# Graph layers in seven-tile chunks over pairs of PSUM banks instead of half chunks in five banks

## The chip, the core and the metric

The kernel runs on one core of a Trainium2 chip. The metric is the device time of one execution in microseconds. Five engines work side by side, each in the order of its own queue, and wait for each other by semaphores: PE (matmuls; its weight loads are listed as PEld), ACT, DVE, POOL and SP, which here only issues transfers.

## What is computed

6250 nodes of 128 features pass through a layer norm, a graph attention layer and three message-passing layers over 200000 edges. The change concerns the three layers:

```python
for i in range(3):
    msg = relu(x[src] + edge_attr)
    aggr = segment_sum(msg, dst, num_segments=6250)
    h = x + aggr
    h = relu(batch_norm(h @ W1[i] + b1[i]))
    h = batch_norm(h @ W2[i] + b2[i])
    x = relu(h) if i != 2 else h
```

## The kernel before

**Tiling.** The nodes stand in 49 blocks of 128. Most edges, sorted by target, form 36 groups. A stage ahead of the layers gives each edge of a group a slot by the block of its source, so that a group is 49 tiles of 128 slots, one tile for each source block, and all its targets lie in one window of 128 nodes. Seven tiles are a chunk, seven chunks a group. A chunk is worked on in two halves, of four and of three tiles; half h belongs to chunk h // 2. The last edges do not go this way: they form 69 units of 7 x 128 edges, about two units to a group, whose source rows POOL gathers one by one.

**A chunk, step by step.** SP loads the attributes of the slots into SBUF (the tile is called `sums`).

- The copy (`seed`, ACT, line 1158) puts the attributes of a half into a PSUM bank.
- The gather (`gather`, PE, line 2049) adds the rows of x: three matmuls to a tile, one for each bf16 part of x, with a one-hot of the sources.
- The relu (`message`, ACT, line 1166) writes the message from PSUM to SBUF.
- The rest (`split_message`, DVE, line 1692) subtracts that from the relu in PSUM, so that the message stands in two parts. In layer one (n = 0) chunks 1, 3 and 5 go without it: there the message is kept whole.
- The one-hot of the targets (`point_targets`, DVE, line 1685) compares an iota with `dl_slot`. The iota stands in PSUM bank 5.
- The sum (`sum_half`, PE, line 2073, or 2076 for whole messages) multiplies message and one-hot, summed over the group in bank 7.

At the group's end ACT copies the window from bank 7 (line 1173), PE turns it (line 2087), and DVE adds it to the nodes (line 1701).

**A unit.** POOL sends seven indirect gathers (line 941), paced by a count of finished sums; DVE adds attributes and rows (line 1715) and makes a one-hot (line 1708); ACT does the relu (line 1178); PE sums (line 2097), in fourteen recorded matmuls; DVE adds the window (line 1722). A table of half numbers says after which half each engine does this.

**What sets the order.** The order is written out by hand in a `group_of` for each engine; groups 2 to 34 run in a hardware loop. A bank is reused by the half that `BANK` puts there next, four, five or seven halves later. ACT runs `message(h)` and then `seed(h + 3)`; PE runs the gather of half h + 3 (at h = 0 those of halves 3 and 4, and none at h = 1) and then the sum of half h. A copy waits until the bank's last user is through (its rest, or its relu for a whole message). A relu also waits until the place in SBUF for its message was emptied by the sum of the chunk that had it.

In layer one DVE also makes the one-hots of the sources (line 1678), three chunks ahead, and POOL scatters sixty late tiles of attributes (line 884) between its gathers; in layers two and three the source one-hots come back from memory by SP.

## Time and profile before

| | us |
|---|---|
| median of three runs | 5063.85 (5047.44 to 5081.66) |
| span of the profiled execution | 4090.3 |
| layer one, from 1838 to 2592 us of the span | 754 |
| layer two, from 2639 to 3319 us | 680 |
| layer three, from 3372 to 4044 us | 672 |

The span runs from the first to the last instruction of one profiled execution. Busy time counts an engine's instructions; an operation's end can overlap the start of the next on the same engine. In a row of the timeline, "x21" is a run of 21 instructions, and the square brackets say how long the engine stood idle before it and what ended that. In a row of groups the time behind the bar is the idle time before the group, with its releasers; "issue" is time in which the engine waited for nothing that the profile shows. PEclk is the granted clock of PE as a share of 2.4 GHz. The rows that are used stand further down.

### The profile page before, as it was taken

Reading aid. Unit: us, or ns where it says so; the run is one execution under the profiler, and the core shown is the slowest. Engines: PE = TensorE matmul, PEld = TensorE weight load, DVE = VectorE, ACT = ScalarE, POOL = GpSimd, SP = SyncE. Lnnn points to the kernel's source line nnn. Section 1 sums busy time; section 2 is a strip of 40 time slices with the busy share of each in tenths; the row PEclk is TensorE's granted clock in tenths of the full one; section 3 lists DMA queues with packets and bytes.
Section 4 is the critical chain, followed back from the end, with each engine's and each line's share of the span. In section 5 each row is a group of like instructions: output and inputs, shape, how many; then the busy total and the mean of one; then the engine's idle time right before and its main releaser. Section 6 shows DMA issues by size and latency. Waiting matters only on the chain.

```text
span 4090.3 us, 151537 instructions
## 1 busy us (share of the span) xinstructions
PE 3879.3 (95%) x50507; PEld 3753.5 (92%) x50510; DVE 3556.7 (87%) x6832; ACT 3072.5 (75%) x7847; POOL 2859.0 (70%) x2594
## 2 busy tenths in 40 slices
PE   3899997999999999989999999899999989999998
PEld 3899996999999999979999999699999969999996
DVE  7799985777777777779999999799999989999997
ACT  4799994677777777777777777678888867887886
POOL 0288885777777777756777777277777736777773
PEclk7788888999999999999999999899999999999999
DMA  9989889998888888868999999589999958999995
GB/s 140 216 291 305 286 277 297 234 248 253 247 250 250 253 247 250 247 211 293 337 338 334 333 329 333 171 300 310 323 310 318 317 176 288 318 319 311 314 316 186
DMA packets 710002, 1132.45 MB, mean 277 GB/s; under 512 B 157402, under 2 KB 535084, under 8 KB 709564
## 3 DMA queue, kind: packets, MB, share of 16 engines
q1 hardware_dynamic: 493068, 787.26, 57.5%
q10 hardware_dynamic: 133200, 176.14, 17.7%
q0 software_dynamic: 83552, 166.66, 12.7%
q8 instruction: 110, 1.80, 0.2%
q14 instruction: 72, 0.59, 0.0%
HBM read 883.83 MB, written 246.33 MB: 276 GB/s over the span
## 4 chain that ended last, share of the span: by engine, by line
PE 84%; DVE 5%; DMA 3%; issue 2%; ACT 2%; SPq 2%; POOL 1%; ACTq 0%; DVEq 0%; PEld 0%; POOLq 0%
PE ps L2049 20%; PE ps L1955 15%; PE ps L2073 14%; PE ps L1942 12%; PE ps L2097 7%; PE ps L2076 4%; PE ps L1883 2%; PE ps L1903 2%; PE ps L1904 2%; PE ps L1891 2%; DMA unit_x<-gin_rows,unit_src 2%; PE ps L2144 2%; PE ps L2087 1%; POOL unit_x L941 1%; DMA h_rows<-att 1%
## 5 line engine op out<-in xcount | busy, mean ns | idle before, releaser
L941 POOL DMA_INDIRECT unit_x<-gin_rows,unit_src x1449 | 1446.6, 998 | 487.8 <-issue 318.4
L878 POOL DMA_INDIRECT attr_by_slot<-abuf,ridx x1020 | 1286.0, 1261 | 455.9 <-issue 308.5
L2049 PE MATMUL ps<-x_parts,src_turned 128*128 128x128 bf16 x15876 | 1137.0, 222 | 21.5 <-ACT ps L1158 18.5
L2049 PEld LDWEIGHTS ps<-x_parts,src_turned 128*128 128x128 fp8e4 x15876 | 948.6, 99 | 67.8 <-issue 25.3
L1158 ACT ACTIVATE ps<-sums 128x512 f32<-128x512 f32 x1512 | 825.8, 546 | 125.9 <-DVE all_split_msg L1692 70.7
L1066 ACT ACTIVATE val<-ps,val 128x128 f32<-128x128 f32 x2597 | 717.9, 375 | 182.6 <-DVE val L1519 182.6
L1685 DVE TENSOR_TENSOR dst_hot<-ps,dl_slot 128x896 fp32r<-128x896 f32 x756 | 817.8, 1082 | 3.5 <-issue 0.4
L1955 PE MATMUL ps<-val,src_hot 128*128 128x129 f32 x5194 | 691.6, 282 | 3.0 <-ACT val L1066 2.5
L2073 PE MATMUL ps<-all_split_msg,dst_hot 128*128 128x256 f32 x3528 | 648.8, 304 | 13.2 <-DVE all_split_msg L1692 12.6
L1166 ACT ACTIVATE all_split_msg<-ps 128x512 fp32r<-128x512 f32 x1008 | 543.7, 539 | 146.0 <-PE ps L2049 113.7
L1692 DVE SCALAR_TENSOR_TENSOR all_split_msg<-ps,all_split_msg 128x512 fp32r<-128x512 f32 x1008 | 609.1, 617 | 14.0 <-ACT all_split_msg L1166 11.5
L1955 PEld LDWEIGHTS ps<-val,src_hot 128*128 128x128 f32 x5194 | 617.5, 192 | 3.7 <-ACT val L1066 2.8
L1942 PE MATMUL ps<-h_win,turned_hot 128*128 128x130 bf16 x7791 | 583.6, 221 | 24.3 <-DVE turned_hot L1445 18.6
L1942 PEld LDWEIGHTS ps<-h_win,turned_hot 128*128 128x128 bf16 x7791 | 502.5, 97 | 30.5 <-issue 19.1
L2073 PEld LDWEIGHTS ps<-all_split_msg,dst_hot 128*128 128x128 f32 x3528 | 479.1, 191 | 17.9 <-issue 10.1
L1944 PE MATMUL ps<-s_parts,turned_hot 128*128 (+1 forms) x2597 | 433.8, 167 | 0.0
L1511 DVE TENSOR_TENSOR src_hot<-iota_one,low 128x768 f32<-128x768 f32 (+1 forms) x441 | 415.7, 943 | 0.0
L2097 PE MATMUL ps<-unit_hot,unit_attr 128*128 128x64 f32 x2898 | 345.7, 271 | 0.0
L2097 PEld LDWEIGHTS ps<-unit_hot,unit_attr 128*128 128x128 f32 x2898 | 341.0, 192 | 0.0
L1507 DVE TENSOR_REDUCE z<-ps 128x6 f32<-128x24 f32 (+1 forms) x490 | 83.6, 179 | 252.6 <-PE ps L1944 251.6
L1445 DVE TENSOR_SCALAR turned_hot<-turned_hot,lane_one 128x1536 bf16<-128x1536 bf16 (+1 forms) x441 | 267.4, 606 | 17.5 <-DMA turned_hot<-rows_by_block 17.5
L1715 DVE TENSOR_TENSOR unit_attr<-unit_attr,unit_x 128x896 f32<-128x896 f32 x207 | 225.8, 1091 | 37.6 <-DMA unit_x<-gin_rows,unit_src 37.2
(268 smaller groups left out, 5787.5 us busy)
## 6 DMA issues: line engine op xcount, KB each, us to landing
sums<-attr_by_slot SPq DMA_DIRECT2D x756, 448.0 KB
turned_hot<-rows_by_block ACTq DMA_DIRECT2D x392, 384.0 KB
attr_by_slot<-zeros SPq DMA_DIRECT2D x36, 3136.0 KB
unit_attr<-in_edge_attr SPq DMA_DIRECT2D x204, 448.0 KB
abuf<-in_edge_attr SPq DMA_DIRECT2D x68, 960.0 KB
src_turned<-src_hots SPq DMA_DIRECT2D x504, 112.0 KB
src_row<-rows_by_group SPq DMA_DIRECT2D x252, 112.0 KB
src_hots<-src_turned SPq DMA_DIRECT2D x252, 112.0 KB
```

The source lines that it names most:

```text
L878: pool.indirect_dma_start(out=attr_table, out_offset=bass.IndirectOffsetOnAxis(ap=ridx[:, g, t0 + t:t0 + t + 1], axis=0), in_=abuf[:, k % ...
L941: pool.indirect_dma_start(out=unit_x[:, half_place(k), t, :], out_offset=None, in_=gin_rows[n], in_offset=bass.IndirectOffsetOnAxis(ap=uni ...
L1066: ins = act.activation(val[:, slot, t, 0:D], given(slot, t)[:, 0:D], ACT.Copy, scale=val[:, slot, t, D:SUM])
L1158: act.activation(ps[:, BANK[h], 0:tiles * D].rearrange("p (b d) -> p b d", d=D), attr[:, first:first + tiles, :], ACT.Copy).then_inc(s_see ...
L1166: act.activation(to, ps[:, BANK[h], 0:tiles * D].rearrange("p (b d) -> p b d", d=D), ACT.Relu).then_inc(s_msg, 1)
L1685: vec.tensor_tensor(dst_hot[:, HOT[c], :, :], iota_ps.unsqueeze(1).to_broadcast([P, G_TILES, P]), dl.rearrange("p o b -> p (o b)").unsquee ...
L1692: vec.scalar_tensor_tensor(split_msgs[n][:, SPLIT_PLACES[n][c], 1, inner, :], ps[:, BANK[h], 0:tiles * D].rearrange("p (b d) -> p b d", d= ...
L1942: pe.matmul(to[:, 0:ROW], turned_hot[:, 0, at:at + P], window_of(g)[:, part * ROW:(part + 1) * ROW], start=(t % 3 == 0 and part == 0), sto ...
L1955: ins = pe.matmul(ps[:, 6, 0:SUM], src_hot[:, slot, t, :], val[:, slot, t, :], start=(c == 0 and t == 0), stop=(c == A_CHUNKS - 1 and t == ...
L2049: ins = pe.matmul(ps[:, BANK[h], k * D:(k + 1) * D], src_turned[:, b * P:(b + 1) * P], x_parts[:, part, b, :], start=False, stop=(k == til ...
L2073: ins = pe.matmul(ps[:, 7, 0:2 * D].rearrange("p (k d) -> p k d", d=D), dst_hot[:, HOT[c], b % G_TILES, :], split_msgs[n][:, SPLIT_PLACES[ ...
L2097: ins = pe.matmul(ps[:, 6, 0:U_WINDOW], unit_attr[:, half_place(k), t, :], unit_hot[:, half_place(k), t, :], start=(t == 0), stop=(t == ti ...
```

## The change

A chunk is no longer halved on its way through PSUM. It lies across two neighbouring banks, and three such pairs take turns by `PAIR`: chunks 0 to 6 use pairs 0, 1, 2, 0, 1, 2, 1, so that chunk 6 follows chunk 4 in pair 1, and chunk 1 of the next group follows chunk 6. Copy, relu and rest become one operation of 896 columns each. PE gathers a whole chunk, two chunks ahead; the sum still runs in two halves, but waits once for the whole chunk, and the unit of a chunk and the turning of the window still stand between or behind these halves. The six banks leave none for the iota, so both one-hots (targets and units) read it from SBUF.

```diff
-BANK = (4, 2, 3, 0, 1, 2, 3, 4, 0, 1, 2, 3, 0, 1)
-IOTA_BANK = 5
+PAIR = (0, 1, 2, 0, 1, 2, 1)
 HOT = (0, 1, 2, 3, 0, 1, 2)
...
-G_LEAD = 3
-AHEAD = ((3, 4), ()) + tuple((h + G_LEAD,) for h in range(2, G_HALVES))
-SEED_LEAD = 3
+G_LEAD = 2
...
-RELU_AT = {6: 0, 13: 1}
+RELU_AT = {3: 0, 6: 1}
...
-WINDOW_OUT_AT = 2
+WINDOW_OUT_AT = 1
...
+        def chunk_ps(c):
+            return ps[:, 2 * PAIR[c]:2 * PAIR[c] + 2, :].rearrange("p b e -> p (b e)")[:, 0:G_TILES * D]
...
+                def seed(i, c):
+                    act.wait_ge(s_attr[c], 16 * (n * BUCKETS + i + 1 + cleared(c)))
+                    before = pair_user(c)
                     if not (isinstance(i, int) and i == 0 and before < 0):
-                        if before % G_HALVES // 2 in SPLITS[n]:
+                        if before % G_CHUNKS in SPLITS[n]:
                             act.wait_ge(s_low, lows_done(n, i, before))
                         else:
-                            act.wait_ge(s_msg, halves_before + G_HALVES * i + before + 1)
-                    act.activation(ps[:, BANK[h], 0:tiles * D].rearrange("p (b d) -> p b d", d=D), attr[:, first:first + tiles, :], ACT.Copy).then_inc(s_seed, 1)
+                            act.wait_ge(s_msg, chunks_done + G_CHUNKS * i + before + 1)
+                    act.activation(chunk_ps(c), attr[:, parts_of(c), :].rearrange("p b d -> p (b d)"), ACT.Copy).then_inc(s_seed, 1)
...
+                def message(i, c):
+                    act.wait_ge(s_gath, chunks_done + G_CHUNKS * i + c + 1 + G_CHUNKS)
+                    act.wait_ge(s_used, halves_before + G_HALVES * i + 2 * place_user(n, c) + 2 + G_HALVES)
...
+                    act.activation(to.rearrange("p b d -> p (b d)"), chunk_ps(c), ACT.Relu).then_inc(s_msg, 1)
...
-                    for h in range(G_HALVES):
...
+                        message(i, c)
+                        if c == WINDOW_OUT_AT and not (isinstance(i, int) and i == 0):
                             keep_window(i - 1)
...
+                        if c + G_LEAD < G_CHUNKS:
+                            seed(i, c + G_LEAD)
                         elif more:
...
+                            seed(i + 1, c + G_LEAD - G_CHUNKS)
...
-                    vec.tensor_tensor(dst_hot[:, HOT[c], :, :], iota_ps.unsqueeze(1).to_broadcast([P, G_TILES, P]),
+                    vec.tensor_tensor(dst_hot[:, HOT[c], :, :], iota_one[:, :].unsqueeze(1).to_broadcast([P, G_TILES, P]),
...
+                def split_message(i, c):
+                    vec.wait_ge(s_msg, chunks_done + G_CHUNKS * i + c + 1)
...
+                    vec.scalar_tensor_tensor(low_of, chunk_ps(c), 0.0, hi, ALU.max, ALU.subtract).then_inc(s_low, 1)
...
-                    vec.tensor_tensor(unit_hot[:, half_place(k), 0:tiles, :], iota_ps[:, 0:U_WINDOW].unsqueeze(1).to_broadcast([P, tiles, U_WINDOW]),
+                    vec.tensor_tensor(unit_hot[:, half_place(k), 0:tiles, :], iota_one[:, 0:U_WINDOW].unsqueeze(1).to_broadcast([P, tiles, U_WINDOW]),
...
-                        if c in SPLITS[n]:
-                            split_message(i, h)
+                        if h % 2 == 0 and c in SPLITS[n]:
+                            split_message(i, c)
...
-                        for k in AHEAD[h]:
...
+                        if h % 2 == 0 and h // 2 + G_LEAD < G_CHUNKS:
+                            gather(i, h // 2 + G_LEAD)
+                        elif h % 2 == 0 and more:
+                            gather(i + 1, h // 2 + G_LEAD - G_CHUNKS)
                         sum_half(i, h)
```

**ACT, the end of a group in the loop of layer three.** Lines with ACTIVATE are the operations; `rows_gathered` counts gathers, `message_rest_ready` rests, `message_used` sums; `slots_cleared_then_slot_attr_loaded1` says that chunk 1's attributes are loaded, and `ps<-sums` is a copy, `all_split_msg<-ps` a relu. Before (relu of half 12, copy of half 1 of the next group, relu of half 13, copy of half 2, relu of the unit):

```order
L1166 ACTIVATE all_split_msg<-ps 128x512 [waits message_used,rows_gathered]
L1155 REGISTER_ALU
L1158 ACTIVATE ps<-sums 128x384 [waits message_rest_ready]
L1163 REGISTER_ALU
L1166 ACTIVATE all_split_msg<-ps 128x384 [waits message_used,rows_gathered]
L1155 REGISTER_ALU [waits slots_cleared_then_slot_attr_loaded1]
L1158 ACTIVATE ps<-sums 128x512 [waits message_rest_ready]
L1177 REGISTER_ALU
L1178 ACTIVATE unit_attr<-unit_attr 128x896 [waits unit_raw_ready]
L1211 REGISTER_ALU
L1211 COMPARE_AND_BRANCH
```

Now (relu of chunk 6, copy of chunk 1 of the next group, relu of the unit; the loop then begins again, with the relu of chunk 0):

```order
L1157 REGISTER_ALU
L1158 REGISTER_ALU [waits rows_gathered]
L1160 ACTIVATE all_split_msg<-ps 128x896 [waits message_used]
L1151 REGISTER_ALU [waits slots_cleared_then_slot_attr_loaded1]
L1154 ACTIVATE ps<-sums 128x896 [waits message_rest_ready]
L1171 REGISTER_ALU
L1172 ACTIVATE unit_attr<-unit_attr 128x896 [waits unit_raw_ready]
L1204 REGISTER_ALU
L1204 COMPARE_AND_BRANCH
```

The copy that stood here for half 2 waited for the rest of half 11; the copy of chunk 1 waits for the rest of chunk 6, whose relu stands one row of work ahead of it, and the unit's relu and the next chunk's relu stand behind it.

**PE around the unit of chunk 4, same loop.** `attributes_in_bank` counts copies, and `h_windows_loaded6` says here that chunk 6's source one-hots are loaded. Before (gather of half 11, sum of half 8, the unit):

```order
L2041 REGISTER_ALU
L2049 MATMUL ps<-x_parts,src_turned 128x128 [waits attributes_in_bank]
L2049 MATMUL ps<-x_parts,src_turned 128x128 x8
L2057 REGISTER_ALU
L2061 REGISTER_ALU [waits message_rest_ready]
L2073 MATMUL ps<-all_split_msg,dst_hot 128x256 [waits dst_hot_ready]
L2073 MATMUL ps<-all_split_msg,dst_hot 128x256 x3
L2095 REGISTER_ALU [waits unit_added,unit_hot_ready,unit_message_ready]
L2097 MATMUL ps<-unit_hot,unit_attr 128x64 [waits window_added]
L2097 MATMUL ps<-unit_hot,unit_attr 128x64 x6
```

Now (gather of chunk 6, first half of sum 4, the unit, second half of sum 4):

```order
L2028 REGISTER_ALU [waits h_windows_loaded6]
L2037 MATMUL ps<-x_parts,src_turned 128x128 [waits attributes_in_bank]
L2037 MATMUL ps<-x_parts,src_turned 128x128 x20
L2046 REGISTER_ALU
L2049 REGISTER_ALU [waits message_rest_ready]
L2061 MATMUL ps<-all_split_msg,dst_hot 128x256 [waits dst_hot_ready]
L2061 MATMUL ps<-all_split_msg,dst_hot 128x256 x3
L2083 REGISTER_ALU [waits unit_added,unit_hot_ready,unit_message_ready]
L2085 MATMUL ps<-unit_hot,unit_attr 128x64 [waits window_added]
L2085 MATMUL ps<-unit_hot,unit_attr 128x64 x6
L2061 MATMUL ps<-all_split_msg,dst_hot 128x256 x3
```

The gather of chunk 6 stands ahead of all of sum 4. Before, the gather ahead of sum 4 was that of half 11, the second of chunk 5, and chunk 6's two gathers (halves 12 and 13) stood behind the unit, ahead of the sums of halves 9 and 10.

**DVE, the one-hots and rests of chunks 4 and 5, same loop.** Before (one-hot of chunk 4, rest of half 8, the unit's one-hot, rest of half 9, one-hot of chunk 5 behind):

```order
L1685 ISA [waits message_used]
L1685 TENSOR_TENSOR dst_hot<-ps,dl_slot 128x896
L1691 REGISTER_ALU
L1692 SCALAR_TENSOR_TENSOR all_split_msg<-ps,all_split_msg 128x512 [waits message_ready]
L1706 REGISTER_ALU
L1708 ISA [waits unit_used]
L1708 TENSOR_TENSOR unit_hot<-ps,unit_dl 128x448
L1691 REGISTER_ALU
L1692 SCALAR_TENSOR_TENSOR all_split_msg<-ps,all_split_msg 128x384 [waits message_ready]
L1684 REGISTER_ALU
L1685 ISA [waits message_used]
L1685 TENSOR_TENSOR dst_hot<-ps,dl_slot 128x896
```

Now (one-hot of chunk 4, rest of chunk 4, the unit's one-hot, one-hot of chunk 5 behind):

```order
L1678 ISA [waits message_used]
L1678 TENSOR_TENSOR dst_hot<-iota_one,dl_slot 128x896
L1682 REGISTER_ALU
L1684 SCALAR_TENSOR_TENSOR all_split_msg<-ps,all_split_msg 128x896 [waits message_ready]
L1697 REGISTER_ALU
L1699 ISA [waits unit_used]
L1699 TENSOR_TENSOR unit_hot<-iota_one,unit_dl 128x448
L1677 REGISTER_ALU
L1678 ISA [waits message_used]
L1678 TENSOR_TENSOR dst_hot<-iota_one,dl_slot 128x896
```

The rest stands at the place of its first half, and both one-hots read `iota_one`, which lies in SBUF, in place of `ps`.

## Rows read from the trace of the kernel before

**Rows 1.** The page's first row: span and number of instructions.

```profile
span 4090.3 us, 151537 instructions
```

**Rows 2.** Stretches, the layers: length; busy PE, PEld, DVE, ACT, POOL; clock, DMA, GB/s.

```profile
1838.00:2592.00 754.00, 745.61 (x8923) 730.58 (x8924) 694.84 (x1041) 551.68 (x1117) 555.09 (x550) 0.99 0.94 325
2639.00:3319.00 680.00, 664.68 (x8168) 644.97 (x8168) 652.61 (x1007) 544.04 (x1117) 489.39 (x490) 0.99 0.90 307
3372.00:4044.00 672.00, 659.18 (x8107) 638.92 (x8107) 646.99 (x1000) 538.76 (x1107) 490.38 (x489) 0.99 0.89 304
```

**Rows 3.** Line 1701, layer two, fourteen window adds: min/median/max ns, first and last start.

```profile
L1701 DVE TENSOR_TENSOR agg<-agg,ps x14: 273/274/285, 2862.1 to 3102.2; 128x128 f32 x14
```

**Rows 4.** Groups by line, layer two, POOL: busy, mean ns, idle before, its releasers.

```profile
L941 POOL DMA_INDIRECT unit_x<-gin_rows,unit_src x483 | 480.7, 995 | 166.8 <-issue 103.6 <-PE ps L2073 62.0 <-DVE unit_attr L1715 1.2
```

**Rows 5.** Timeline, layer two, PE: start us, length us, operation, count.

```profile
3002.17 1.67 PE L2097 MATMUL ps<-unit_hot,unit_attr 128*128 128x64 f32 x14
3003.67 1.34 PE L2049 MATMUL ps<-x_parts,src_turned 128*128 128x128 bf16 x21
3004.82 1.07 PE L2073 MATMUL ps<-all_split_msg,dst_hot 128*128 128x256 f32 x7
3005.73 0.68 PE L2049 MATMUL ps<-x_parts,src_turned 128*128 128x128 bf16 x9
3006.22 0.72 PE L2073 MATMUL ps<-all_split_msg,dst_hot 128*128 128x256 f32 x4
3006.78 0.84 PE L2049 MATMUL ps<-x_parts,src_turned 128*128 128x128 bf16 x12
...
3007.87 0.68 PE L2049 MATMUL ps<-x_parts,src_turned 128*128 128x128 bf16 x9
```

**Rows 6.** Groups by line and form, layer two, ACT.

```profile
L1158 ACT ACTIVATE ps<-sums 128x512 f32<-128x512 f32 x252 | 151.1, 600 | 34.6 <-DVE all_split_msg L1692 34.5
L1166 ACT ACTIVATE all_split_msg<-ps 128x512 fp32r<-128x512 f32 x252 | 148.9, 591 | 38.0 <-PE ps L2049 19.6 <-issue 15.8
L1158 ACT ACTIVATE ps<-sums 128x384 f32<-128x384 f32 x252 | 124.6, 494 | 0.0
L1166 ACT ACTIVATE all_split_msg<-ps 128x384 fp32r<-128x384 f32 x252 | 122.9, 488 | 36.0 <-PE ps L2049 34.3 <-issue 1.7
L1178 ACT ACTIVATE unit_attr<-unit_attr 128x896 f32<-128x896 f32 x69 | 65.3, 947 | 14.9 <-DVE unit_attr L1715 14.8
```

**Rows 7.** Timeline, layer two, DVE.

```profile
3000.74 1.08 DVE L1685 TENSOR_TENSOR dst_hot<-ps,dl_slot 128x896 fp32r<-128x896 f32 x1
3001.74 1.15 DVE L1692 SCALAR_TENSOR_TENSOR all_split_msg<-ps,all_split_msg 128x512 fp32r<-128x512 f32 x2
3002.80 1.08 DVE L1685 TENSOR_TENSOR dst_hot<-ps,dl_slot 128x896 fp32r<-128x896 f32 x1
...
3005.42 1.08 DVE L1685 TENSOR_TENSOR dst_hot<-ps,dl_slot 128x896 fp32r<-128x896 f32 x1
...
3007.15 1.08 DVE L1715 TENSOR_TENSOR unit_attr<-unit_attr,unit_x 128x896 f32<-128x896 f32 x1
```

**Rows 8.** Timeline, layer two, POOL, two gathers in succession.

```profile
3005.94 0.95 POOL L941 DMA_INDIRECT unit_x<-gin_rows,unit_src  x1 [0.31 <-PE ps L2073]
3007.19 1.86 POOL L941 DMA_INDIRECT unit_x<-gin_rows,unit_src  x1 [0.30 <-PE ps L2073]
```

**Rows 9.** Attention stage, 750 to 1810 us: three groups by line, one timeline row.

```profile
L878 POOL DMA_INDIRECT attr_by_slot<-abuf,ridx x776 | 820.8, 1058 | 236.5 <-issue 236.5
...
L1511 DVE TENSOR_TENSOR src_hot<-iota_one,low 128x768 f32<-128x768 f32 x364 | 348.9, 959 | 0.0
L1445 DVE TENSOR_SCALAR turned_hot<-turned_hot,lane_one 128x1536 bf16<-128x1536 bf16 x362 | 222.1, 613 | 0.0
...
1207.36 0.96 POOL L878 DMA_INDIRECT attr_by_slot<-abuf,ridx  x1 [0.30 <-issue]
```

**Rows 10.** Groups by line, layer one, DVE: the one-hot of the sources.

```profile
L1678 DVE TENSOR_SCALAR src_turned<-src_row,lane_one 128x896 fp8e4<-128x896 uint8 x251 | 176.5, 703 | 2.4 <-DMA src_row<-rows_by_group 2.0 <-issue 0.5
```

126 lines of the change are left out of this document (48 added, 78 removed).

## The prediction

> **What bounds the kernel now.** I took the whole time first, then the three layers, then what each engine does in one group. The profiled execution spans 4090.3 us [rows 1]; the median of the runs is 5063.85 us, so 973.5 us lie around the span, and I leave them unchanged. The three layers fill 754, 680 and 672 us of the span [rows 2]; the change touches nothing else, apart from a few waits before them.
>
> In the layers PE is busy 98 to 99% of the time, DVE 92 to 96%, ACT 73 to 80%, at a granted clock of 0.99, the 2.4 GHz level [rows 2]. A group of the second layer takes (3102.2 - 2862.1) / 13 = 18.5 us [rows 3]. DVE works 652.6 / 36 = 18.1 us of it: two engines are nearly full, so no wait of DVE can be hidden for long.
>
> POOL looks idle and is not. In layer two it sends 483 gathers (14 in a full group) of 0.995 us on average [rows 4], and 0.3 us passes before each, even when nothing is waited for [rows 9]: 14 x 1.30 = 18.2 us of 18.5 in a full group. Of the 166.8 us that it stood idle before them, 483 x 0.3 = 145 are this step; 22 us in the whole layer are room. In layer one two scatters of late edges come on top: 16 operations of 1.01 us (555.09 / 550 [rows 2]) and 0.3 make 20.9 us, which is all of 754 / 36 = 20.9.
>
> **The change, part by part.** I write g for the 21 gather matmuls of a chunk, S for its rest on DVE, P for its one-hot on DVE, and a number for the chunk.
>
> *PE, a gain.* No matmul is added or removed. A gather of 21 with its sum of 7 takes 3005.73 - 3003.67 = 2.06 us; the same work as 9, 4, 12 and 3 takes 3007.87 - 3005.73 = 2.14 [rows 5]. Before, one chunk of a group already runs whole, so the gain is 6 x 0.08 = 0.48 us a group, 52 us over 108 groups; in layer one it may be less. This holds only if PE stays the bound.
>
> *ACT, less work.* From 384 to 512 columns an operation grows by 0.106 us (copy) and 0.103 us (relu) [rows 6]. Three more such steps give 0.92 and 0.90 us for 896 columns. The row of an 896-wide relu, 0.947 us, bounds a whole operation in one piece. No row shows one across two banks; if the crossing cost a second start, the price would be that of the two halves of now, 1.09 and 1.08 us, and nothing would be gained. ACT works about 2.5 us a group less, but it was not full: nothing on the path, except where DVE waits for it.
>
> *DVE, about 0.4 us a group less.* Two halves of S run as a pair in 1.15 us. A P of 896 takes 1.08 us, and its successor starts 1.00 us after it [rows 6, 7]. I price S like P: 0.06 to 0.07 us saved per chunk. DVE's own work becomes 18.1 - 0.4 = 17.7 us a group. The copy of the iota into PSUM, once a layer, is worth under 1 us.
>
> *A wait at the end of the group.* Chunk 1 of the next group uses the same pair as chunk 6. ACT stands in order: relu 6, copy 1' (waits for S6), relu of the unit, relu 0'. DVE runs S6, P0, S0, and S0 needs relu 0'. From the end of S6: copy 0.92, unit relu 0.95, relu 0.90, and 0.03 at either end for a semaphore (an estimate), less twice the 0.08 by which an operation of DVE overlaps the next [rows 7], which I take for ACT too: 2.7 us. DVE has only P0 to put there, 1.0 us. It waits 1.7 us. Behind S0 in DVE's queue stand all further one-hots and rests, and PE needs those. Before, the copy at that place waited for the rest of half 11 and not of half 13.
>
> *A wait in the middle.* Chunk 6 uses the pair of chunk 4, and relu 6 also needs the message place that sum 4 empties. In layers two and three, from the end of S4: copy 6 with its semaphores 0.98, g6 1.15, first four of sum 4 0.56, the unit's fourteen 1.50 (they stand between the halves of sum 4), last three 0.5 (three sevenths of a sum's 1.07), relu 6 0.90, semaphores 0.06: 5.7 us until S6 can start [rows 5, 6]. DVE's own work there is a unit one-hot (half as wide as P, an estimate of 0.55), P5, S5, P6 and the unit's add: 4.6 us. It waits 1.1 us. In layer one chunk 6's place was last used by chunk 2, so this wait is absent.
>
> Sum for layers two and three: 17.7 + 1.7 + 1.1 = 20.5 us a group in place of 18.5. That is 2.0 x 36 = 72 us a layer, 144 for both. PE's 18.0 us of work fits inside. In layer one DVE's 694.8 / 36 = 19.3 [rows 2], less 0.2 for four chunks merged, with 2.7 - 1.0 - 0.7 = 1.0 of wait (a source one-hot of 0.70 us fills part [rows 10]), makes 20.1: under the 20.9 of now, so the order costs nothing there.
>
> *The iota back in SBUF.* P and the unit's one-hot read dl_slot or unit_dl from SBUF already, so now both inputs lie in SBUF. DVE itself pays nothing: the unit's add, with both inputs in SBUF, takes the same 1.08 us [rows 7]. POOL pays. A gather takes 0.95 us; one that began 0.04 us after such an add took 1.86 us, and ended 0.82 us after the add did [rows 7, 8]. It was held until DVE was done. The gather before it began 0.52 us after a P and took 0.95: with the iota in PSUM, P holds nobody.
>
> The Trainium skill ("SBUF — State Buffer", "Who interferes with whom") states that a DVE operation with two SBUF inputs contends with a GpSimd instruction that reads SBUF, and that the one issued second fully blocks; it speaks against this edit. The trace agrees for the add; that it also holds for the new P, no row of this kernel's layers shows.
>
> Seven P of 1.08 and two unit one-hots of 0.55 make 8.7 us a group in which a gather can now be held, 42% of 20.5. The price per gather is bounded from two rows. Upper end: a gather falls at random and waits half an operation, 0.42 x 0.5 = 0.21 us. Lower end: in the attention stage POOL also runs without pause, next to a one-hot of the very form P now has and a second one-hot of 0.61 us, together (348.9 + 222.1) / 1060 = 54% of the time; its scatters average 1.058 us against 0.96 free [rows 9]. That is 0.10 us at 54%, so 0.08 at 42%. For 14 gathers: 1.1 to 2.9 us, so POOL needs 19.3 to 21.1 us a group. The sum of the waits, 20.5, lies inside: POOL's delay runs beside them, and I add nothing for it there.
>
> Layer one has no wait of order to cover it, and POOL nothing to spare. Its 16 operations with 0.08 to 0.21 more (8.7 of 20.9 is the same share) need 1.3 to 3.4 us a group. I take 1.6, nearer to the lower end, whose row has the same form of one-hot: 1.6 x 36 = 58 us, from 47 to 122.
>
> *Sum:* 144 + 58 = 202 us. The span becomes 4292, the time 5064 + 202 = 5266 us.
>
> **The rivals.**
>
> 1. *POOL becomes the bound.* Where DVE runs S and P without a pause, a held gather ends 0.82 us after P, and the next starts 0.3 later, 1.12 after P's end. By then the next P runs (S takes 1.0), so POOL is held again: one gather a chunk instead of two, until DVE pauses. Its 18.2 of 18.5 us speak for this, the attention stage against it, where a larger share cost it only 0.10 us. At the upper end layers two and three take 21.1 us (2.6 x 36 = 94 each) and layer one 122: +310, 5374 us. If one gather a group more is lost, at 1.25 us, for which DVE's add then waits, that is 135 us on top: 5509.
>
> This rival is the rule of the Trainium skill ("SBUF — State Buffer", "Who interferes with whom") taken as the bound; the add's row agrees with its mechanism, and no row yet with its size here.
>
> 2. *The pipeline closes up and PE stays the bound: not slower.* One mechanism decides it: whether copy 1' and copy 6 find their pair free by the time PE has other work. DVE would have to be 1.7 us ahead at the end of the group. Its load of 96% speaks against it: it idles 27 us in a whole layer [rows 2]. If it is so, the gain of PE stands: -52, 5012 us. POOL must then fit in 18 us too, which needs a price under 0.05 per gather.
>
> 3. *The waits are half as long,* since a full chunk of lead lets DVE catch up in the stretch between S0 and S4, and POOL pays the lower end: 72 + 47 = +119, 5183 us.
>
> **How the numbers follow.** The waits of order as summed, with POOL beside them: 0.46 (5200 to 5330). Rival 1: 0.26. Rival 3: 0.15, with a tail towards no change. Rival 2: 0.13, half of it below -1%, since -52 us is just about that. A measurement of this kernel tells about 1% (51 us) from no change. Faster by over 1% (below 5013): 0.06. Within 1%: the other half of rival 2 and a quarter of rival 3, 0.11. Slower: 0.83. The range runs from 5100, in the tail of rival 3, to 5420, in the upper half of rival 1; rival 2 and the ends of the other two, 0.2 in all, lie outside.
>
> **What would show it.** Right: groups of layers two and three about 20.5 us apart; PE busy well under 98% there; DVE's rest waiting for ACT's relu about 36 times a layer for over 1 us, and ACT's copy waiting for the rest; gathers at 1.08 us or more. Also right: a gather of 21 and a sum of 7 still 2.06 us. Wrong: PE at 98% again (rival 2), or DVE's unit add waiting for gathers most of all, with POOL idle for nothing but its 0.3 (rival 1). Were the 896-wide operations much dearer over two banks than 1.08 and 0.95 us, the sum would fail from the other side.

## The result and the profile after

The changed kernel takes 5346.66 us (median of 4 runs, 5334.68 to 5376.3), the kernel before 5061.52 (4 runs, 5047.44 to 5081.66) on the same chip: 1.057 times as long, with an interval of 1.052 to 1.062. That is 285 us more, where the prediction had 202, and inside its range.

Its profiled execution spans 5339.4 us, which is nearly its whole time. The profile of before that stands ahead of the prediction spans 4090.3 us [rows 1] of a time of some 5060. A second profile of the same kernel before, taken for this study, spans 5011.8 us in a run of 5013.5. So nothing of size lies around the span there. The time of the execution behind the first profile is not on record; by its rows it was faster than any that was timed. From here on, "the kernel before" is this second profile, and [rows 2 to 4] are kept for what they led to.

The three layers of the second profile of before, by windows (length; busy time and count of PE, PEld, DVE, ACT, POOL; granted clock, DMA share, GB/s):

```profile
2260.00:3200.00 940.00, 813.28 (x8958) 747.68 (x8959) 720.88 (x1067) 559.11 (x1129) 561.32 (x550) 0.99 0.85 264
3250.00:4090.00 840.00, 719.26 (x8024) 653.30 (x8023) 658.74 (x1007) 536.35 (x1098) 480.79 (x483) 0.98 0.74 244
4140.00:4980.00 840.00, 720.33 (x8068) 654.87 (x8067) 662.28 (x1012) 537.68 (x1102) 483.66 (x485) 0.98 0.74 244
```

And of the changed kernel:

```profile
2280.00:3273.00 993.00, 822.51 (x8939) 791.68 (x8939) 701.12 (x904) 516.67 (x626) 651.17 (x555) 0.91 0.81 251
3330.00:4285.00 955.00, 774.65 (x8097) 744.06 (x8095) 651.44 (x749) 502.62 (x609) 533.23 (x490) 0.87 0.65 218
4340.00:5300.00 960.00, 778.13 (x8119) 744.76 (x8118) 657.11 (x758) 505.64 (x614) 527.51 (x490) 0.87 0.65 216
```

DVE, ACT and POOL of the kernel before work about as long as in [rows 2], PE 8% longer (719 us for 665), and this in layers that are 160 us longer: PE is busy 86% of the second layer and DVE 78%, not 98 and 96. No engine is full. With the change PE is busy 81%, DVE 68%, and the clock granted is 0.87 in place of 0.98.

The window adds of layer two give the length of a group, as [rows 3] did: first the kernel before, then the changed one (count; min/median/max ns; first and last start).

```profile
L1701 DVE TENSOR_TENSOR agg<-agg,ps x36: 275/278/290, 3263.7 to 4073.7; 128x128 f32 x36
```

```profile
L1692 DVE TENSOR_TENSOR agg<-agg,ps x36: 277/289/291, 3362.9 to 4285.8; 128x128 f32 x36
```

(4073.7 - 3263.7) / 35 = 23.1 us a group before, (4285.8 - 3362.9) / 35 = 26.4 after: 3.2 us more. The groups by line and shape of the changed kernel in layer two, of ACT, DVE and POOL (busy us, mean ns; idle before, its releasers), answer to [rows 4, 6, 7]:

```profile
L1154 ACT ACTIVATE ps<-sums 128x896 f32<-128x896 f32 x249 | 228.8, 919 | 150.9 <-DVE all_split_msg L1684 113.5 <-issue 37.4
L1160 ACT ACTIVATE all_split_msg<-ps 128x896 fp32r<-128x896 f32 x251 | 228.7, 911 | 286.9 <-PE ps L2061 192.5 <-PE ps L2037 48.9 <-remote 40.7
...
L1684 DVE SCALAR_TENSOR_TENSOR all_split_msg<-ps,all_split_msg 128x896 fp32r<-128x896 f32 x251 | 273.3, 1089 | 136.3 <-ACT all_split_msg L1160 112.6 <-issue 21.4 <-DVE agg L1731 0.8
L1678 DVE TENSOR_TENSOR dst_hot<-iota_one,dl_slot 128x896 fp32r<-128x896 f32 x250 | 271.5, 1086 | 0.0
...
L939 POOL DMA_INDIRECT unit_x<-gin_rows,unit_src x483 | 524.8, 1087 | 401.0 <-PE ps L2061 247.8 <-issue 81.3 <-remote 65.6
```

Copy 0.919, relu 0.911, rest 1.089, one-hot 1.086, gather 1.087: each price of the prediction is met. What is new stands behind the second bar. Copies wait for the rest, relus for the sums, the rest for relus.

PE's side of layer two, kernel before first, gives the whole account:

```profile
L2049 PE MATMUL ps<-x_parts,src_turned 128*128 128x128 bf16 x5154 | 380.9, 221 | 51.7 <-issue 45.3 <-ACT ps L1158 3.9
L2073 PE MATMUL ps<-all_split_msg,dst_hot 128*128 128x256 f32 x1730 | 324.7, 308 | 48.9 <-issue 24.4 <-DVE all_split_msg L1692 15.1 <-ACT window_out L1173 8.6
L2097 PE MATMUL ps<-unit_hot,unit_attr 128*128 128x64 f32 x966 | 121.2, 272 | 13.9 <-issue 13.5
```

```profile
L2037 PE MATMUL ps<-x_parts,src_turned 128*128 128x128 bf16 x5229 | 386.2, 236 | 169.1 <-ACT ps L1154 147.5 <-issue 20.9
L2061 PE MATMUL ps<-all_split_msg,dst_hot 128*128 128x256 f32 x1759 | 325.3, 322 | 7.9 <-issue 5.6 <-DVE all_split_msg L1684 2.2
L2085 PE MATMUL ps<-unit_hot,unit_attr 128*128 128x64 f32 x966 | 149.3, 321 | 0.0
```

The window of layer two is 115 us longer. PE idles 60 of them: by these rows 117 more before gathers, which wait for the copy of attributes, and 55 less before sums and unit sums. The other 55 are busy time (774.65 - 719.26): the same unit sum takes 321 ns a matmul where it took 272. The two windows end differently, so here is the stretch from the first to the last window add as well, kernel before first:

```profile
3263.70:4073.70 810.00, 695.08 (x7851) 636.77 (x7849) 638.31 (x971) 521.86 (x1068) 473.68 (x476) 0.98 0.75 249
3362.90:4285.80 922.90, 750.56 (x7823) 721.29 (x7821) 629.60 (x728) 483.29 (x585) 515.86 (x475) 0.87 0.65 217
```

113 us more, of which 57 are idle time of PE and 55 busy time, for as many matmuls within 0.4%. The clock records of the trace say where the busy time comes from: in this stretch the change was granted 1.2 GHz for 246 us, in 49 pieces, the kernel before for 31 us, in five.

Some of the growth is the chip's. The second profile of before comes from a chip on which its run took 5013.5 us, the change from one on which the kernel before takes 5061.5: 1% more, about 8 us a layer.

One group shows both halves. The timeline of the changed kernel at chunk 6 (start, length, operation, idle before):

```profile
3602.89 0.29 DVE L1692 TENSOR_TENSOR agg<-agg,ps 128x128 f32 x1 [2.03 <-remote]
...
3603.12 1.09 DVE L1678 TENSOR_TENSOR dst_hot<-iota_one,dl_slot 128x896 fp32r<-128x896 f32 x1
3604.13 1.08 DVE L1684 SCALAR_TENSOR_TENSOR all_split_msg<-ps,all_split_msg 128x896 fp32r<-128x896 f32 x1
...
3605.25 0.92 ACT L1154 ACTIVATE ps<-sums 128x896 f32<-128x896 f32 x1 [2.30 <-issue]
...
3606.32 2.40 PE L2037 MATMUL ps<-x_parts,src_turned 128*128 128x128 bf16 x21 [2.67 <-ACT ps L1154]
...
3608.47 1.20 PE L2061 MATMUL ps<-all_split_msg,dst_hot 128*128 128x256 f32 x4
...
3609.47 3.08 PE L2085 MATMUL ps<-unit_hot,unit_attr 128*128 128x64 f32 x14
...
3612.31 0.99 PE L2061 MATMUL ps<-all_split_msg,dst_hot 128*128 128x256 f32 x3
...
3612.69 0.22 DVE L1713 TENSOR_TENSOR agg<-agg,ps 128x64 f32 x1 [4.57 <-PE ps L2085]
...
3613.34 0.92 ACT L1160 ACTIVATE all_split_msg<-ps 128x896 fp32r<-128x896 f32 x1 [5.52 <-PE ps L2061]
...
3614.93 1.09 DVE L1684 SCALAR_TENSOR_TENSOR all_split_msg<-ps,all_split_msg 128x896 fp32r<-128x896 f32 x1
3615.93 1.08 DVE L1678 TENSOR_TENSOR dst_hot<-iota_one,dl_slot 128x896 fp32r<-128x896 f32 x1
3616.05 0.92 ACT L1154 ACTIVATE ps<-sums 128x896 f32<-128x896 f32 x1 [1.79 <-DVE all_split_msg L1684]
3616.91 0.93 ACT L1172 ACTIVATE unit_attr<-unit_attr 128x896 f32<-128x896 f32 x1
3617.11 1.33 PE L2037 MATMUL ps<-x_parts,src_turned 128*128 128x128 bf16 x21 [0.70 <-ACT ps L1154]
3617.74 0.90 ACT L1160 ACTIVATE all_split_msg<-ps 128x896 fp32r<-128x896 f32 x1
3618.68 1.09 DVE L1684 SCALAR_TENSOR_TENSOR all_split_msg<-ps,all_split_msg 128x896 fp32r<-128x896 f32 x1 [1.66 <-issue]
```

It is the prediction's chain in the middle, link by link: rest of chunk 4 (3604.13), copy 6, gather 6, four of sum 4, unit sum, three of sum 4, relu 6, rest of chunk 6 (3614.93). PE stood 2.67 us before gather 6; sum 4, ready since 3605.21, stood behind it for the last 1.1 of them. After the stand gather, sum and unit sum take 2.40, 1.20 and 3.08 us, where [rows 5] have 1.34, 0.72 and 1.67: the granted clock is 0.50 from 3606.35 to 3612.30, the 1.2 GHz level. It fell during the stand, at 3605.14, and rose at 3615.38, after PE had worked without a pause from 3606.32 on. DVE stood too: the unit's window add (L1713) waits 4.57 us for the unit sum, and behind it in DVE's queue stand the one-hot, the unit's add and the rest of chunk 6. At the end of the group, rest 6 to rest 0 goes as written too: copy, unit relu, relu, 1.66 us of wait.

### The profile page after: what moved, and what is told of

Its sections match the earlier page's. It is cut to its first block, busy times and chain, and to the rows that moved or that the text cites. A ratio compares the mean times of both kernels' runs of the same rounds, so it can differ in the third digit from the quotient of the medians.

```text
span 5339.4 us, 144524 instructions
## 1 busy us (share of the span) xinstructions
PE 4334.2 (81%) x50515; PEld 4096.5 (77%) x50518; DVE 3557.6 (67%) x6181; ACT 2939.8 (55%) x6335; POOL 2971.5 (56%) x2594
## 4 chain that ended last, share of the span: by engine, by line
PE 51%; issue 15%; DVE 13%; another core or an unknown queue 9%; ACT 7%; DVEq 2%; SPq 1%; DMA 1%; ACTq 1%; PEld 0%
PE ps L2037 13%; PE ps L2061 8%; PE ps L1943 7%; PE ps L2085 7%; PE ps L1930 5%; ACT ps L1154 3%; DVE src_hot L1504 3%; DVE all_split_msg L1684 2%; PE ps L1891 2%; PE ps L1892 2%; PE ps L1871 2%; PE ps L2064 2%; PE ps L1879 2%; DVE turned_hot L1438 1%
## 5 line engine op out<-in xcount | busy, mean ns | idle before, releaser
L939 POOL DMA_INDIRECT unit_x<-gin_rows,unit_src x1449 | 1609.0, 1110 | 1088.6 <-PE ps L2061 601.0
L2037 PE MATMUL ps<-x_parts,src_turned 128*128 128x128 bf16 x15876 | 1151.6, 233 | 501.3 <-ACT ps L1154 384.4
L2037 PEld LDWEIGHTS ps<-x_parts,src_turned 128*128 128x128 fp8e4 x15876 | 1019.6, 105 | 580.7 <-issue 562.1
L1154 ACT ACTIVATE ps<-sums 128x896 f32<-128x896 f32 x756 | 694.4, 919 | 519.8 <-DVE all_split_msg L1684 221.8
L1678 DVE TENSOR_TENSOR dst_hot<-iota_one,dl_slot 128x896 fp32r<-128x896 f32 x756 | 824.2, 1090 | 0.6 <-remote 0.6
L1160 ACT ACTIVATE all_split_msg<-ps 128x896 fp32r<-128x896 f32 x504 | 459.2, 911 | 573.0 <-PE ps L2061 387.7
L1684 DVE SCALAR_TENSOR_TENSOR all_split_msg<-ps,all_split_msg 128x896 fp32r<-128x896 f32 x504 | 548.9, 1089 | 282.9 <-ACT all_split_msg L1160 231.3
L1930 PE MATMUL ps<-h_win,turned_hot 128*128 128x130 bf16 x7791 | 640.7, 224 | 111.7 <-issue 101.5
L2085 PEld LDWEIGHTS ps<-unit_hot,unit_attr 128*128 128x128 f32 x2898 | 441.3, 238 | 1.1 <-issue 1.0
L2085 PE MATMUL ps<-unit_hot,unit_attr 128*128 128x64 f32 x2898 | 436.4, 315 | 0.8 <-issue 0.8
L1058 ACT ACTIVATE z<-z 128x6 f32<-128x6 f32 (+1 forms) x441 | 96.0, 218 | 526.6 <-DVE z L1507 359.0
L1932 PEld LDWEIGHTS ps<-s_parts,turned_hot 128*128 128x128 bf16 x2597 | 260.1, 100 | 50.0 <-issue 48.4
```

The lines of the kernel that those rows point to most:

```text
L939: pool.indirect_dma_start(out=unit_x[:, half_place(k), t, :], out_offset=None, in_=gin_rows[n], in_offset=bass.IndirectOffsetOnAxis(ap=uni ...
L1154: act.activation(chunk_ps(c), attr[:, parts_of(c), :].rearrange("p b d -> p (b d)"), ACT.Copy).then_inc(s_seed, 1)
L1678: vec.tensor_tensor(dst_hot[:, HOT[c], :, :], iota_one[:, :].unsqueeze(1).to_broadcast([P, G_TILES, P]), dl.rearrange("p o b -> p (o b)"). ...
L1684: vec.scalar_tensor_tensor(low_of, chunk_ps(c), 0.0, hi, ALU.max, ALU.subtract).then_inc(s_low, 1)
L1930: pe.matmul(to[:, 0:ROW], turned_hot[:, 0, at:at + P], window_of(g)[:, part * ROW:(part + 1) * ROW], start=(t % 3 == 0 and part == 0), sto ...
L1932: ins = pe.matmul(to[:, ROW:A_COL], turned_hot[:, 1, at:at + P], s1_of, start=False, stop=(t % 3 == 2 or t == a_tiles(c) - 1))
```

## The experiments

A table first, since most verdicts rest on it. The ratio is to the kernel before on the same chip, with its 95% interval; the layers run from first to last window add of a layer, in us, in the profiled execution. The changed kernel, profiled twice, gave 938 and 938, 923 and 930, 917 and 928 us, so a difference of ten says little. The layers are not set against a kernel of the same chip: those of four rows (before, list of lanes, and the two with the unit sum later) come from a chip on which the kernel before takes 4990 us, the others from chips on which it takes 5061 to 5081, so these four are 1 to 2% short beside the rest.

| kernel | ratio, interval | layer one | two | three |
|---|---|---|---|---|
| before, second profile | 1 | 882 | 810 | 807 |
| before, list of lanes in SBUF | 1.007 (1.004-1.011) | 892 | 825 | 822 |
| before, halves in the pairs' banks | 1.003 (1.000-1.006) | 906 | 822 | 823 |
| the same, four halves ahead | 1.010 (1.006-1.015) | 920 | 825 | 832 |
| change, sum first | 1.029 (1.024-1.034) | 952 | 859 | 875 |
| change, sum first, four places | 1.037 (1.030-1.043) | 942 | 856 | 875 |
| change, way in by halves | 1.039 (1.033-1.045) | 980 | 866 | 864 |
| change, four places | 1.045 (1.039-1.052) | 950 | 899 | 899 |
| change, again | 1.062 (1.055-1.069) | 938 | 930 | 928 |
| change, unit sum later | 1.069 (1.064-1.073) | 947 | 920 | 928 |
| change, unit sum later, unit relu first | 1.071 (1.066-1.077) | 960 | 925 | 922 |
| change, way out by halves | 1.081 (1.074-1.087) | 983 | 971 | 973 |

### The kernel before, again

No edit.

> The kernel before, profiled once more, because the changed kernel's profile spans 5339 us, the whole of its time, while that of before spanned 4090 of 5064. If the profile of before was an execution unlike the timed ones, this one spans about 5060 us, and its attention stage, which the change does not touch, about 1480 us as in the changed kernel, not 1060. If 973 us do lie around the span of before, it spans 4090 again.

One run: 5013.5 us, span 5011.8, at a granted clock of 0.937 over the whole. Its groups of layer two are 23.1 us apart. Everything below is compared with this.

### Only the list of lanes goes to SBUF

```
-  iota_ps.unsqueeze(1)          # point_targets; the same in point_unit
+  iota_one[:, :].unsqueeze(1)
```

> The kernel before, with one edit of the change alone: both one-hots read the iota from SBUF. POOL theory (held gathers are the loss): most of the change's 285 us come with it, 5250 us or more, and gathers grow from about 1.00 to 1.1 us or more. Order theory (the loss is the waits at reused pairs): at most 60 us, out of layer one, 5060 to 5120 us.

5027.09 us, against 4989.61 for the kernel before on this chip: 1.007. That is in the range of the order theory (5060 to 5120 of 5061.5, so 1.000 to 1.012), and far from the POOL theory's 1.037 and more. The gathers of POOL in all three layers, kernel before and then this one (busy, mean ns; idle before):

```profile
L941 POOL DMA_INDIRECT unit_x<-gin_rows,unit_src x1449 | 1440.9, 994 | 971.1 <-PE ps L2073 391.9 <-issue 246.4 <-remote 194.6
```

```profile
L941 POOL DMA_INDIRECT unit_x<-gin_rows,unit_src x1449 | 1629.8, 1125 | 820.6 <-issue 302.5 <-PE ps L2073 294.6 <-remote 148.2
```

A gather takes 0.131 us more, inside the prediction's 0.08 to 0.21, and 189 us in all. But 971 us of idle time stood before them, and the kernel loses some 37. Layer one grows by 10 us, not by 58 (the layers together by 39). So the hold is real and its effect small: POOL was not full. The trace also shows how strictly POOL is held. Of the gathers that begin while a P runs, 417 here, 415 end 0.82 to 0.85 us after that P's end, as the prediction's one row behind the unit's add did; they take 1.36 us on average. In the kernel before, with the iota in PSUM, such gathers take 0.97, and their ends keep no distance to the P (80% of them 0.27 to 0.71 us after it).

### Unit sum later, and unit relu ahead of the copy

```
-SUM_AT = {8: 0, 13: 1}
+SUM_AT = {9: 0, 13: 1}          # both kernels
+if c == 6 and unit_at(RELU_AT, i, c) is not None:   # the second kernel only:
+    message_of_unit(i, unit_at(RELU_AT, i, c))      # ahead of seed(i + 1, ...)
```

> The changed kernel, with the unit's sum behind the whole sum of chunk 4 instead of between its halves; the relu of the unit stays. Order theory: the wait in the middle, 1.06 us a group in layers two and three, goes: 5347 - 76 = 5271 us. POOL theory: unchanged, 5330 to 5350 us.

> The changed kernel, with two waits of the order taken out: the unit's relu stands ahead of the copy for chunk 1 at the end of a group, and the unit's sum behind the whole sum of chunk 4. Order theory: the wait at the group's end falls by 0.85 us and that in the middle by 1.06, 1.9 x 72 groups = 137 us: 5347 - 137 = 5210 us. POOL theory: POOL's gathers remain the bound, 5330 to 5350 us.

5327.51 and 5352.2 us, 1.069 and 1.071: no gain in either. The times expected are for a chip on which the kernel before takes 5061.5 us. As ratios, the order theory's 5271 and 5210 are 1.041 and 1.029, the POOL theory's 5330 to 5350 are 1.053 to 1.057, and both runs lie above both. The change itself was not run on this chip. Two waits of the prediction were shortened, that of relu 6 for the unit sum and that of rest 0 for the unit relu, and nothing came back. The waits of the second kernel, all layers (us, times, longest), beside the 384.4 and 387.7 us of the change for the same two pairs:

```profile
PE ps L2039 <- ACT ps L1154: 424.6, 187, 4.4
ACT all_split_msg L1160 <- PE ps L2063: 352.9, 205, 2.5
```

The relus wait less for sums, and the gathers more for copies. The second kernel is no clean removal: in its new place the unit's relu waits 364.3 us for the unit's add on DVE (98 times). As far as the two runs go, the waits on DVE, on which the prediction's sum was built, are not the ones that set the length: PE's is.

### Four kernels on one chip: the change, the banks, the way out, the places

The changed kernel itself:

> The changed kernel itself, beside the kernel before on this chip, as the mark for the other three runs. Both theories below: 1.05 to 1.07 of before, with relu waiting for sums of PE for some 390 us and gathers waiting for the copy for some 380 us in the three layers.

5374.98 us, 1.062.

The kernel before, nothing merged, in the banks of the pairs:

```
-BANK = (4, 2, 3, 0, 1, 2, 3, 4, 0, 1, 2, 3, 0, 1)
-IOTA_BANK = 5
+BANK = (0, 1, 2, 3, 4, 5, 0, 1, 2, 3, 4, 5, 2, 3)
```

> The kernel before, with its half operations, but the halves laid in the six banks of the three pairs as the change lays its chunks (half 0 of a chunk in the first bank of its pair, half 1 in the second), and the list of lanes in SBUF since its bank is taken. Nothing is merged. Grain theory (the loss comes from whole-chunk operations that hand over to each other, where halves overlapped): 1.00 to 1.015 of before, that is the 0.7% of the list in SBUF and nothing else, groups of layer two about 23.5 us apart. Placement theory (the loss comes from which bank follows which: chunk 6 in chunk 4's pair, chunk 1 in chunk 6's): 1.04 to 1.06, groups near 26 us, copies of halves 12 and 2 waiting for the rest.

5080.0 us, 1.003. With halves, which bank follows which, and the list in SBUF with it, cost next to nothing: the placement theory falls. The loss of the change needs whole chunks, in the lead, the way in or the way out.

The way out of a chunk in halves again:

```
+    if k in (FIRST - 1, G_TILES - 1):
         ins.then_inc(s_gath, 1)                 # gather reports twice
-    act.activation(to.rearrange(...), chunk_ps(c), ACT.Relu)
+    for h in (2 * c, 2 * c + 1): ... act.activation(to, half_ps(h), ACT.Relu)
-    split_message(i, c)                         # at even h
+    split_message(i, h)                         # at every h; sum_half waits by half
```

> The changed kernel with the way out of a chunk in halves again: the gather reports after 12 and after 21 matmuls, and relu, rest and the wait of the sum are by halves; the copy of attributes, the order of gathers and sums and the pairs stay as in the change. Costs ACT and DVE about 0.2 us more a chunk (two times 0.49 to 0.60 for 0.92). Grain theory: the hand-over relu, rest, sum shrinks by about 1 us wherever it is waited for, twice a group and more: 1.02 to 1.04 of before, groups of layer two 24 to 25 us. Placement theory: no gain, 1.05 to 1.07.

5481.46 us, 1.081: worse, against both theories. The copy that opens a reused pair waits for the second half of the rest, which now ends later, behind two relus and two rests (about 0.2 us dearer a chunk each). In the trace ACT idles 747.6 us before copies where the change has 531.7. But the edit does more than halve: the second half of a rest goes back to DVE's odd step, and at two chunks of a group an add stands between the halves that waits for PE, the window add at chunk 3 and the unit's window add at chunk 5. In all layers DVE waits 302.6 us before window adds and 391.0 us before the units' window adds, where the change has 120.3 and 333.5. How much of the loss is this order and how much the halves, no run shows.

Four message places (the fourth lies in SBUF where layer one keeps its source rows; only the lines of the order are shown):

```
-SPLIT_PLACES = (..., ) + 2 * ({0: 0, 1: 1, 2: 2, 3: 0, 4: 1, 5: 2, 6: 1},)
+SPLIT_PLACES = (..., ) + 2 * ({0: 0, 1: 1, 2: 2, 3: 3, 4: 0, 5: 1, 6: 2},)
```

> The changed kernel with four places for split messages in layers two and three in place of three (places 0, 1, 2, 3, 0, 1, 2 for chunks 0 to 6), so that no relu waits for the sum of the chunk two before it, but for one three or four before. Everything else is the change's. Message theory (the 390 us for which relu waits for sums are on the path): 100 us less than the change, 1.03 to 1.04. Grain theory and placement theory: the relu then waits for the gather, or the copy for the rest, and no more than 20 us come back, 1.05 to 1.07.

5292.22 us, 1.045: some 83 us less than the change beside it, nearer to the message theory's 100 than to the others' 20. Relu 6, which waited 5.52 us in the timeline above, no longer waits for sum 4.

### Sum first

```
+late = PAIR_SINCE[ahead % G_CHUNKS] == G_LEAD       # chunk 6, and 1 of the next group
+if late:
+    sum_half(i, h)
+if h % 2 == late and ahead < G_CHUNKS:
     gather(i, ahead)
 ...
+if not late:
+    sum_half(i, h)
```

> The changed kernel with one order turned round on PE, at the two places of a group where a chunk's pair was used by the chunk two before it (chunk 6 after 4, chunk 1 of the next group after 6): there the sum of the chunk that has just been split runs ahead of the gather two chunks on, not behind it. Nothing else is changed. Lead theory (the gather two chunks ahead waits for rest, copy and their hand-over while the finished chunk's sum stands behind it on PE, in whole chunks where the kernel before reached only three halves ahead): PE has 0.9 us of sum and at chunk 4 a unit sum of 1.5 us to do in the wait of two hand-overs, so about 1 to 1.5 us twice in 36 groups and three layers, 200 to 300 us less if nothing else takes its place: 1.00 to 1.03 of before. Operation theory (the whole-chunk copy, relu and rest themselves are too long a chain, whatever PE's order): no more than 50 us less, 1.05 to 1.06.

5225.49 us, 1.029: of the 6.2 points that the change cost on the chip of the four kernels, 3.3 are gone (2.8 of the 5.7 of its first measurement). That is some 140 to 165 us where the lead theory wanted 200 to 300: its mechanism holds, its size falls short, and 1.029 is the edge of its range. Timeline at the same place as above:

```profile
3623.05 1.08 DVE L1684 SCALAR_TENSOR_TENSOR all_split_msg<-ps,all_split_msg 128x896 fp32r<-128x896 f32 x1
...
3624.17 0.92 ACT L1154 ACTIVATE ps<-sums 128x896 f32<-128x896 f32 x1 [2.27 <-DVE all_split_msg L1684]
3624.27 0.74 PE L2061 MATMUL ps<-all_split_msg,dst_hot 128*128 128x256 f32 x4 [1.68 <-DVE all_split_msg L1684]
...
3624.84 1.67 PE L2085 MATMUL ps<-unit_hot,unit_attr 128*128 128x64 f32 x14
...
3626.32 0.60 PE L2061 MATMUL ps<-all_split_msg,dst_hot 128*128 128x256 f32 x3
...
3626.76 2.52 PE L2037 MATMUL ps<-x_parts,src_turned 128*128 128x128 bf16 x42
```

Sum 4 starts 0.14 us after its rest, the unit sum runs in 1.67 us, and gather 6 finds its copy long done (42 matmuls are two gathers on end). In layer two the gathers idle 3.0 us for copies:

```profile
L2037 PE MATMUL ps<-x_parts,src_turned 128*128 128x128 bf16 x5166 | 370.3, 232 | 34.7 <-issue 31.3 <-ACT ps L1154 3.0
L2061 PE MATMUL ps<-all_split_msg,dst_hot 128*128 128x256 f32 x1732 | 307.4, 312 | 101.5 <-issue 56.3 <-DVE all_split_msg L1684 40.4 <-ACT window_out L1167 3.9
```

Layers two and three lose 71 and 53 us of their length, layer one nothing (952 us). The wait has moved more than it has gone, since the sums now idle 101.5 us for 7.9. From first to last window add of layer two, to be set against the rows above:

```profile
3346.60:4206.10 859.50, 721.43 (x7818) 678.57 (x7818) 623.09 (x729) 481.11 (x585) 518.34 (x475) 0.91 0.71 233
```

Beside the first profile of the change, PE idles 34 us less and is busy 29 us less for the same matmuls, at a granted clock of 0.91 for 0.87. DVE's wait for the unit sum falls from 315.4 us in all layers to 35.9.

With four places as well:

> The kernel above, with the four places for split messages in layers two and three as well, which alone took some 80 us off the change. Lead theory: the two waits lie at the same two places (chunk 6 and chunk 1) and are partly one, so 20 to 60 us less than the order alone: 0.99 to 1.02 of before. Operation theory: the 80 us of the places alone and little more, 1.04 to 1.045.

5255.71 us, 1.037, no better than sum first alone, and outside what either theory gave, by a little on the operation theory's side. The 83 us of the places were another way to the same time, not more of it.

### As far ahead with halves

```
-G_LEAD = 3
+G_LEAD = 4                      # SEED_LEAD too; AHEAD one half a step
```

> The kernel before with its halves in the six banks of the three pairs (which alone was 1.003 of before), and copies and gathers four halves ahead in place of three, as far ahead as the change's two chunks; the pair of gathers that stood together at a group's start goes back to one a half. All operations stay halves. Lead theory: the gather of half 12 then waits for the rest of half 8 and that of half 2 for half 12, which have only just been split, while their sums stand behind it; a half's hand-over is shorter than a chunk's, so 1.02 to 1.05 of before. Operation theory: lead does no harm in halves, 0.99 to 1.01.

5132.21 us, 1.010, against 1.003 three halves ahead. The lead theory gave 1.02 to 1.05, so lead by itself, in halves, costs under 1%. The waits of the change do appear (gathers wait 244.3 us for copies, against 384.4 in the change), but they are shorter (1.4 us on average for 2.0), and the time shows that most of them find cover.

### Way in by halves, way out by chunks

```
-G_LEAD = 2                                   # chunks
+G_LEAD = 3                                   # halves; copies and gathers in halves
+BANK = tuple(2 * p + k for p in PAIR for k in range(2))
...
```

> The changed kernel with the way into a chunk as it was before the change: copies of attributes and gathers in halves, three halves ahead, each half waiting for its own bank of the pair; the way out stays as changed, with relu, rest and the wait of the sum once a chunk (the relu waits for both gathers of its chunk). Lead theory: what is left of the loss once the sum runs first at two places (2.9% of before) also comes from copies and gathers that reach two whole chunks ahead, and relu and rest in one operation cost nothing: 0.99 to 1.01 of before, layers two and three near the 823 us each of the halves in pairs (first to last window add). Operation theory: half of the loss is in the longer relu and rest, with the sum behind them: 1.02 to 1.04, layers two and three 850 us or more.

5257.02 us, 1.039, layers two and three 866 and 864 us: the operation theory's side. With banks, list and lead as in the second kernel of the four, relu and rest once a chunk, with what hangs on them in the order (both copies behind a whole relu, the sum behind a whole rest), cost 3.6 points: 74, 43 and 40 us in the layers. The relus and rests of split messages, first with halves in the pairs' banks (both halves in a row), then here:

```profile
L1164 ACT ACTIVATE all_split_msg<-ps 128x512 fp32r<-128x512 f32 x1008 | 545.2, 541 | 473.6 <-remote 271.9 <-PE ps L2046 193.8 <-PE ps L2070 2.8
L1690 DVE SCALAR_TENSOR_TENSOR all_split_msg<-ps,all_split_msg 128x512 fp32r<-128x512 f32 x1008 | 620.0, 622 | 259.9 <-issue 156.7 <-ACT all_split_msg L1164 93.8 <-DVE agg L1738 1.5
```

```profile
L1164 ACT ACTIVATE all_split_msg<-ps 128x896 fp32r<-128x896 f32 x504 | 460.5, 914 | 584.6 <-PE ps L2042 395.4 <-remote 159.1 <-PE ps L2066 22.3
L1689 DVE SCALAR_TENSOR_TENSOR all_split_msg<-ps,all_split_msg 128x896 fp32r<-128x896 f32 x504 | 550.0, 1091 | 449.5 <-ACT all_split_msg L1164 323.2 <-issue 121.6 <-DVE agg L1736 1.5
```

The idle time before them grows by 111 and 190 us. (The releasers alone mislead here, since much of the waiting with halves stands under "remote" and "issue".) A relu can start only when all 21 matmuls of its chunk are done, and the rest only behind 0.91 us of relu; in halves the second relu runs beside the first rest.

Where PE pays for it, the sums of layer two show, first to last window add, in the same order:

```profile
L2070 PE MATMUL ps<-all_split_msg,dst_hot 128*128 128x256 f32 x1697 | 320.6, 308 | 43.2 <-DVE all_split_msg L1690 22.8 <-issue 18.4 <-ACT window_out L1171 0.9
L2066 PE MATMUL ps<-all_split_msg,dst_hot 128*128 128x256 f32 x1690 | 327.7, 315 | 78.4 <-ACT window_out L1171 56.8 <-DVE all_split_msg L1689 8.7 <-issue 6.9
```

They wait 56.8 us for the copy of the window, which empties bank 7 for the next group and stands on ACT behind the whole relu of chunk 1 (before, behind that of its first half). With halves it was 0.9; in layer three the two are 60.4 and 1.1 us. So in layers two and three much of this run's loss may lie in the place of that one copy; no run moved it.

No version beats the kernel before.

## Why the prediction was right in sign, and what failed in it

**The time around the span** failed first. The 973.5 us are inside, by the second profile. With groups of 23.1 us in place of 18.5 PE, DVE and POOL were not nearly full, and every argument that began with "DVE has no room" or "POOL is 18.2 of 18.5" had the wrong base. The sign did not hang on it: the waits come from the order of handing over.

**Prices of single operations** held: copy 0.919 (0.92), relu 0.911 (0.90), rest 1.089 (1.08), a merged gather and sum 2.07 us at the high clock (from one gather's start at 3593.78 to the next one's at 3595.85; forecast 2.06). PE's gain of 52 us is not seen, by its own condition: PE was not full (81% of layer two).

**The wait at the end of the group** was right link by link: 2.66 us from the end of rest 6 to rest 0 (forecast 2.7), DVE waiting 1.66 (1.7); the 0.03 us for a semaphore, an estimate there, is 0.03 and 0.04 in these rows (rest 6 ends at 3616.02, copy 1' starts at 3616.05). But it was charged to the length of the group, and the run that shortened it gained nothing. By the waits that grew in its place, it lay beside PE's own.

**The wait in the middle** is the term that was mis-sized. Forecast: 5.7 us from the end of rest 4 to rest 6, of which DVE would wait 1.1. In the group shown it is 3614.93 - 3605.21 = 9.7 us. Gather, four of sum, unit sum and three of sum at the low clock account for 3.3 of the 4.0 us of difference: 3613.30 - 3606.32 = 7.0 against the 3.7 that was summed. Most of the rest is DVE's order: P6 and the unit's add were to fill DVE's wait, but they stand behind the unit's window add, which the prediction left out and which waits 4.57 us for the unit sum, so that S6 starts 0.7 us after relu 6 has ended. I had the right chain and priced it with DVE as the engine that pays; PE pays, since gather 6 blocks the sum behind it, and it pays twice, in standing and in running slower afterwards. Turning that one order round, here and for chunk 1, gave back about 3 points (2.8 or 3.3, by the two measurements of the change). The forecast for both waits was 72 us a layer in layers two and three. The layers grew by 113 and 110 (some 8 of each the chip's); turning the order gave back 71 and 53.

**What was missing** is the grain of the way out. I set the chunk-wide relu and rest at a small gain for ACT and DVE (2.5 and 0.4 us a group), since their time is shorter than two halves'. With the way in left in halves they cost 74, 43 and 40 us in the layers, with what hangs on them. That all layers, the first too, lose by it speaks against "in layer one the order costs nothing"; in the change itself that layer was not taken apart.

**The iota in SBUF:** mechanism and price per gather right (0.131 us; forecast 0.08 to 0.21), the 58 us in layer one wrong: 10 of it are seen when only the list is moved. The Trainium skill ("SBUF — State Buffer", "Who interferes with whom") is borne out in its mechanism by that run, in which a gather that begins during a P ends 0.82 us after it. Layer one did grow, by 56 us in the first profile of the change, and its near agreement with the forecast is chance.

The sum of 202 us is thus partly luck: 58 in layer one for POOL, where 10 are seen, and nothing for the grain and the clock. The parts measured do not add up either (way in by halves and way out by halves, each alone, leave 1.039 and 1.081; both together 1.003); a wait that is removed uncovers another. Of the rivals, POOL as bound is refuted by its 401 us of idle time in layer two; PE as bound and half-sized waits by groups 3.2 us longer. DVE's rest did wait for relu, 119 times in layer two, for 112.6 us, and 47 times for over 1 us, where the prediction had said about 36; the copy waited for the rest 54 times, for 113.5 us, as it had also said.

What stays open: 2.9% are left with the sum first. Its whole-chunk way out could explain them, by the run that kept only that, but no run had the way out in halves together with the sum first, and the one run that halved the way out of the change lost by it. Nor did a run move the copy of the window. Layer one was not taken apart.

## What to carry to other kernels

Merging two halves into one operation saves the fixed cost of one and gives up their overlap: count the hand-overs from engine to engine in the loop that frees a buffer, not the busy time. On an engine that works in order, put the work that is ready ahead of the work that waits for a buffer just being freed. And see first that the profile is of an execution like those timed: a span 20% under the median means that the busy shares read from it are too high.
